# Two-layer gated cross attention with experts: value products joined per key tile, maxima as single evenly placed units, exponentials 800 columns wide

## The reference

```python
x = x + tanh(g_xattn[0]) * L0_xattn(layernorm(x), ctx, ctx, mask)     # 16 heads of 8, masked softmax
x = x + tanh(g_ffn[0])   * L0_ffn(layernorm(x))                       # 64 experts, 8 per token, and a shared one
x = x + tanh(g_xattn[1]) * L1_xattn(layernorm(x), ctx, ctx, energy)   # softmax times a gate per key
x = x + tanh(g_ffn[1])   * L1_ffn(layernorm(x))                       # 8 experts, 2 per token
```

## Time and profile before

| what | us |
|---|---|
| median of 3 runs | 1134.18 (1134.06 to 1135.10) |
| the profiled execution | 1136.61 |
| its span, first to last instruction | 1134.80 |
| TensorE, VectorE, ScalarE busy in it | 1000.3, 821.4, 564.5 |
| opening maxima, layer 0 and layer 1 | 28.0 and 22.5 |
| one batch of attention, layer 0 and layer 1 | 52.6 to 54.2 and 41.6 |

### The profile page before, as it was taken

How to read it: one execution, slowest core, us unless ns; L and a number is a source line. 1 busy time by engine, 2 the same in 40 slices (tenths; PEclk the granted TensorE clock), 3 DMA queues, 4 the chain that set the end, 5 groups by cost and what they waited for, 6 DMA issues and landing times.

```text
span 1134.8 us, 25320 instructions
## 1 busy us (share of the span) xinstructions
PE 1000.3 (88%) x9740; PEld 704.2 (62%) x9740; DVE 821.4 (72%) x1911; ACT 564.5 (50%) x1194; POOL 351.3 (31%) x278
## 2 busy tenths in 40 slices
PE   4889999999999999858999789999999999960997
PEld 2356666666666666548888546666666666540986
DVE  7977776767767675657999797777777677440996
ACT  2034445454544446525666306665655655750664
POOL 6521221212130300005777450441341341000774
PEclk8579999999999999958999859999999999975999
DMA  6522313030303040017655143223313404005662
GB/s 170 103 46 55 76 38 80 28 80 28 80 28 81 1 108 2 2 51 203 172 166 151 36 113 79 67 67 81 82 51 80 97 11 108 2 5 89 181 166 59
DMA packets 48094, 88.57 MB, mean 78 GB/s; under 512 B 21154, under 2 KB 31558, under 8 KB 47974
## 3 DMA queue, kind: packets, MB, share of 16 engines
q1 hardware_dynamic: 47974, 86.96, 31.6%
HBM read 47.24 MB, written 1.75 MB: 43 GB/s over the span
## 4 chain that ended last, share of the span: by engine, by line
PE 56%; DVE 18%; issue 6%; POOL 6%; ACT 4%; DMA 4%; SPq 1%; DVEq 0%; POOLq 0%; ACTq 0%
PE pm L1130 15%; PE po L1176 14%; PE ps L1156 11%; POOL tmpf L775 6%; PE ps L1159 5%; PE pc L1087 4%; DVE junk L416 3%; PE pc L1104 3%; DVE vaug L537 2%; DVE qsel L528 2%; ACT qsel L939 2%; DVE mx_part L419 2%; DMA routing<-vaug 2%; DVE negm L429 2%; DMA wts<-in_experts 1%
## 5 line engine op out<-in xcount | busy, mean ns | idle before, releaser
L851 ACT ACTIVATE probs<-ps 121x400 f32<-121x400 f32 (+1 forms) x768 | 347.7, 503 | 264.0 <-PE ps L1159 168.2
L1130 PE MATMUL pm<-khi,qbd 128*100 128x482 f32 (+5 forms) x653 | 318.5, 496 | 12.1 <-DVE mx_part L416 8.7
L416 DVE CUSTOM_DVE_ANT_0 junk<-pm,negq 100x482 bf16<-100x482 f32 (+1 forms) x360 | 233.3, 658 | 79.3 <-PE pm L1130 58.4
L1156 PE MATMUL ps<-qst,kst 128*121 128x400 f32 (+1 forms) x768 | 259.7, 404 | 5.5 <-ACT probs L851 2.9
L419 DVE TENSOR_REDUCE mx_part<-pm 128x1 f32<-128x482 f32 (+3 forms) x293 | 186.0, 655 | 58.7 <-PE pm L1130 57.4
L1176 PE MATMUL po<-probs,vaug 121*32 121x100 f32 x6144 | 214.2, 258 | 3.9 <-ACT oraw L878 3.9
L1176 PEld LDWEIGHTS po<-probs,vaug 121*32 121x32 f32 x6144 | 128.6, 110 | 116.3 <-issue 99.9
L1130 PEld LDWEIGHTS pm<-khi,qbd 128*100 128x100 f32 (+2 forms) x653 | 115.8, 179 | 86.3 <-issue 42.8
L1156 PEld LDWEIGHTS ps<-qst,kst 128*121 128x121 f32 (+1 forms) x768 | 141.4, 188 | 42.4 <-issue 20.7
L1301 PE MATMUL ps<-qsel,qst 128*128 128x400 f32 x660 | 139.9, 364 | 1.1 <-DVE qst L520 1.1
L775 POOL TENSOR_TENSOR tmpf<-vaug,wb 128x400 f32<-128x400 f32 x55 | 68.6, 1248 | 213.1 <-DMA wb<-routing 151.5
(11 more groups left out here) (179 smaller groups left out, 1011.2 us busy)
## 6 DMA issues: line engine op xcount, KB each, us to landing
kst<-khi SPq DMA_DIRECT2D x128, 180.5 KB, 3.9
wb<-routing SPq DMA_DIRECT2D x66, 200.0 KB, 3.7
ctxT<-in_ctxT SPq DMA_DIRECT2D x16, 722.0 KB, 4.2
kst<-klo SPq DMA_DIRECT2D x64, 180.5 KB, 3.9
wts<-in_experts SPq DMA_DIRECT2D x55, 192.0 KB, 3.7
wb<-routing SPq DMA_DIRECT2D x22, 400.0 KB, 4.0
qsel<-qhi SPq DMA_DIRECT2D x16, 100.0 KB, 2.5
routing<-vaug SPq DMA_DIRECT2D x1, 1100.0 KB
```

The costliest lines, as they stand in the source:

```text
L416: ins = nc.vector.tensor_tensor_reduce(junk[:, k % 2, 0:w], max_bank(b, k)[0:S, 0:w], negq[:, lo:lo + w], 1.0, -3e38, ALU.add, ALU.max, mx ...
L851: nc.scalar.activation(probs[t % 2][0:r, g * GQ:(g + 1) * GQ], ps[0:r, g, 0:GQ], ACT.Exp, scale=SCALE).then_inc(s["probs_ready"], 1)
L1130: nc.tensor.matmul(max_bank(b, k)[0:rows, 0:w], qbd[:, first:first + rows], khi[:, lo:lo + w], start=True, stop=True).then_inc(s["chunk_re ...
L1156: mm = nc.tensor.matmul(ps[0:r, g, 0:GQ], kst[par][:, g, t * KEY_TILE:t * KEY_TILE + r], qst[par][:, g * GQ:(g + 1) * GQ], start=True, sto ...
```

## The change

- `weigh` does a key tile's sixteen value products in one run, behind scores 0 and 1 of the next tile, and waits for all its exponentials.
- The exponential covers two groups, 800 columns, at once (`exp_half`). A score group waits for the half that last used its bank pair.
- The due times go. Maxima are single units: one behind each score, a fifth (if the tile has one) behind the product placed beside. A unit is now (block, third); the thirds start at 0, 482 and 962 and are all 482 wide, and in layer 1 the last block overlaps so that all have 128 rows. All use the two banks of `pm`, those of batch 0 too.
- `khi`, `klo` and `qbd` have two buffers. K of batch b+2 is projected in tiles 4 to 6 of batch b, K of batch 1 among the opening maxima; V in tiles 7 to 9; `turn_out`, `turn_back`, `project` in tiles 1, 2 and 3.
- The sign of the maximum is in `max_mask`; the negation goes. The gate is multiplied into `wo` and, with the bias, into `xres` ahead of the layer's first maximum, and `add_out` is one operation. The semaphore increment ahead of each layer-0 maximum on VectorE goes.

```diff
-MAX_PER_SLOT = [[1, 4, 4, 4, 4, 4, 4, 5, 6, 6, 6, 0], [0, 4, 4, 3, 3, 3, 3, 4, 5, 5, 5, 0]]
+UNITS_PER_SLOT = [[5, 4, 4, 4, 5, 4, 4, 4, 5, 5, 4, 0], [4, 4, 4, 4, 4, 4, 4, 3, 3, 3, 2, 0]]
+TURN_OUT_SLOT, TURN_BACK_SLOT, OUT_SLOT, K_SLOT, V_SLOT, ROW_SLOT = 1, 2, 3, 4, 7, KEY_TILES - 1
+FIRST_K_AFTER, FIRST_K_TAKEN = [7, 15, 23], [11, 19, 27]
...
-                        dve.sem_inc(s["chunk_seen"], 1)
...
-                    nc.vector.tensor_scalar(negm[0:rows, 96:96 + blocks], negm[0:rows, 96:96 + blocks], -1.0, None,
-                                            ALU.mult).then_inc(s["rowmax_step"], 1)
...
+                step(nc.vector.tensor_scalar(wo[l][:], wo[l][:], tgates[:, l:l + 1], None, ALU.mult))
+                step(nc.vector.scalar_tensor_tensor(xres[:], bo[l][0:S, :].unsqueeze(1).broadcast_to([S, B, D]),
+                                                    tgates[0:S, l:l + 1], xres[:], ALU.mult, ALU.add))
...
+                    nc.scalar.activation(probs[t % 2][0:r, 2 * u * GQ:2 * (u + 1) * GQ].rearrange("p (g q) -> p g q", q=GQ),
+                                         ps[0:r, 2 * u:2 * u + 2, 0:GQ], ACT.Exp, scale=SCALE)\
...
+                    if n >= 2:
+
+                        pe.wait_ge(s["max_taken"], n - 1)
+                    first, lo = MAX_FIRST[l][i], MAX_STARTS[c]
+                    nc.tensor.matmul(pm[0:rows, n % 2, 0:MAX_W], qbd[b % 2][:, first:first + rows],
+                                     khi[b % 2][:, lo:lo + MAX_W], start=True, stop=True).then_inc(s["chunk_ready"], 1)
...
-                    pe.wait_ge(s["probs_ready"], b * (G * KEY_TILES) + (G * t + 2 * u + 2))
+                    pe.wait_ge(s["probs_ready"], 2 * (b * KEY_TILES + t) + 2)
...
+                        scores(b, t, 0)
+                        for u in here[0:1]:
+                            max_unit(b + 1, u)
+                        if b < B - 1 and t == ROW_SLOT:
                             max_rows(b + 1)
...
+                        scores(b, t, 1)
+                        for u in here[1:2]:
+                            max_unit(b + 1, u)
+                        if t >= 1:
+                            weigh(b, t - 1)
+                        elif b >= 1:
+                            weigh(b - 1, KEY_TILES - 1)
+                        scores(b, t, 2)
+                        for u in here[2:3]:
+                            max_unit(b + 1, u)
+                        scores(b, t, 3)
+                        for u in here[3:4]:
+                            max_unit(b + 1, u)
+                        beside(b, t)
+                        for u in here[4:]:
+                            max_unit(b + 1, u)
+
+                for u in range(len(units)):
+                    max_unit(0, u)
+                    if u in FIRST_K_AFTER:
+                        k_chunk(1, FIRST_K_AFTER.index(u))
...
-    a["max_mask"] = (row[:, None] - 96 == np.arange(H)).astype(f)
+    a["max_mask"] = -(row[:, None] - 96 == np.arange(H)).astype(f)
...
-    nc = bacc.Bacc("TRN2", target_bir_lowering=False, num_devices=1)
+    nc = bacc.Bacc("TRN2", target_bir_lowering=False, num_devices=1, dynamic_dma_scratch_size=1024)
```

More of the change, by code:

```diff
@@ L184, in flamingo @@
         ctxT = [sb(f"ctxT{i}", [128, NKP]) for i in range(2)]
-        khi = sb("khi", [128, NK], F32R)
-        klo = sb("klo", [128, NK], F32R)
+        khi = [sb(f"khi{i}", [128, NK], F32R) for i in range(2)]
+        klo = [sb(f"klo{i}", [128, NK], F32R) for i in range(2)]
         kst = [sb(f"kst{i}", [128, G, NK], F32R) for i in range(2)]
@@ L193, in flamingo @@
         qst = [sb(f"qst{i}", [128, HQ], F32R) for i in range(2)]
-        qbd = sb("qbd", [128, HQ], F32R)
-        mx_part = sb("mx_part", [128, H, len(CHUNKS)])
+        qbd = [sb(f"qbd{i}", [128, HQ], F32R) for i in range(2)]
+        mx_part = sb("mx_part", [128, H * 3])
         negm = sb("negm", [128, 128])
-        junk = sb("junk", [100, 2, 512], BF16)
+        junk = sb("junk", [100, 2, MAX_W], BF16)
         probs = [sb(f"probs{i}", [KEY_TILE, HQ]) for i in range(2)]
@@ new lines, in unit_max @@
+                def unit_max(b, u):
+                    n, (i, c) = b * len(units) + u, units[u]
+                    bank = pm[0:rows, n % 2, 0:MAX_W]
+                    part = mx_part[0:rows, i * 3 + c:i * 3 + c + 1]
+                    dve.wait_ge(s["chunk_ready"], n + 1)
+                    if l == 1:
+                        nc.vector.tensor_reduce(part, bank, AX, ALU.max).then_inc(s["max_taken"], 1)
+                    else:
+                        nc.vector.tensor_tensor_reduce(junk[:, n % 2, :], bank, negq[:, MAX_STARTS[c]:MAX_STARTS[c] + MAX_W],
+                                                       1.0, -3e38, ALU.add, ALU.max, part).then_inc(s["max_taken"], 1)
@@ L432, in row_max @@
+                def row_max(b):
+                    parts = mx_part[0:rows, 0:blocks * 3].rearrange("p (h c) -> p h c", c=3)
+                    dve.wait_ge(s["max_taken"], (b + 1) * len(units))
+                    nc.vector.tensor_reduce(negm[0:rows, 96:96 + blocks], parts, AX, ALU.max)\
+                        .then_inc(s["rowmax_ready"], 1)
                     dve.wait_ge(s["maxrow_ready"], b + 1)
-                    if not (isinstance(b, int) and b < 2):
-                        dve.wait_ge(s["pv_done"], b * KEY_TILES - KEY_TILES)
@@ L480, in slots @@
-                def slots(b, main, tail, par):
-                    for t in range(KEY_TILES):
-                        if main and t == 0:
-                            k_low(b + 1, 0)
-                        for i, k in enumerate(MAX_SLOTS[l][t]):
-                            chunk_max(b + 1, k)
-                            if i == BESIDE_AFTER.get(t, 0):
-                                beside(b, t, main, tail)
-                        if tail and t == OUT_SLOT:
-                            add_out(b - 1)
-                    row_max(b + 1, 1 - par)
@@ L686, in max_queries @@
                 def max_queries(b):
-                    if not (isinstance(b, int) and b == 0):
-                        pool.wait_ge(s["chunk_ready"], b * (3 * MAX_BLOCKS[l]))
-                    nc.gpsimd.tensor_tensor(qbd[:].rearrange("p (h q) -> p h q", q=S),
+                    if b >= 2:
+                        pool.wait_ge(s["chunk_ready"], (b - 1) * len(MAX_UNITS[l]))
+                    nc.gpsimd.tensor_tensor(qbd[b % 2][:].rearrange("p (h q) -> p h q", q=S),
                                             qhi[:, bass.ds(b * S, S)].unsqueeze(1).broadcast_to([128, H, S]),
@@ L903, in slots @@
                                 router0("a")
-                slots(0, True, False, True, 0)
+                for c in range(len(CHUNKS)):
+                    k_high(1, c)
+                slots(0)
                 if l == 0:
@@ L1291, in attention @@
+                for u in range(len(units)):
+                    max_unit(0, u)
+                    if u in FIRST_K_AFTER:
+                        k_chunk(1, FIRST_K_AFTER.index(u))
+                max_rows(0)
+                for b in range(B):
+                    slots(b)
+                weigh(B - 1, KEY_TILES - 1)
+                turn_out(B - 1)
                 turn_back(B - 1)
```

373 lines of the change are left out of this document (136 added, 237 removed).

## The result

The changed kernel takes **1105.93 us** (median of 4 runs, 1102.24 to 1108.05) against 1134.64 of the kernel before on the same chip: ratio **0.9744**, 95% interval 0.9716 to 0.9771. It is 28.7 us faster, two and a half times the forecast gain of 11.4. That lies inside the range of 1102 to 1140, but outside the 1112 to 1134 that the forecast claimed on its own. The profiled execution is the fastest of the four (span 1100.4) and that of the kernel before is 2 us over its median, so differences of the two traces come out some 6 us too good.

The account below looks back on a forecast made before the run. TensorE's stream was taken to bound the batches and VectorE the openings. Layer 0 at -20.8 us and layer 1 at +9.4 gave net -11.4, so 1123 us; range 1102 to 1140, about 8 in 10, 1112 to 1134 on its own.

Parts of the forecast that it names:

- the openings: Opening stretches: two banks for four +8.1 and +7.2 us, K of batch 1 +4.8 per layer, new operations +2.0 and +1.7.
- the five low clocks of layer 0: Layer-0 batch edges: the low clock behind five row-maxima waits goes, -8.0 us.
- the row wait: Layer-0 batch edges: with the negation gone TensorE waits 0.87 us instead of 1.84, -5.2 us over the layer.
- The slow rival: Layer-1 batches: stops of 0.2 to 0.6 us lower the clock, 1.6 us per drop, 1145 at two per batch; chance 12%.
- The scaling of `wo`: Ahead of VectorE's first maximum: this tensor_scalar beside GpSimd's work could be caught for up to 1.6 us.
- the openings at the full clock: Rival for the opening stretches: 0.62 us per maximum and K at 0.81, -16 us, 1107; chance 12%.
- banks that don't bind: Rival for layer 1: VectorE catches up in the value run, 3.5 us per batch go, 1099; chance 10%.
- the 0.5 that I had put on top for VectorE's start: Layer-0 batches: a further instruction at VectorE's start on a maximum costs 0 to 0.5 us per batch, 0.5 taken.
- banks 3.48: Layer-1 batch: waits for the two maxima banks to turn round, summed over its tiles, lose 3.48 us.
- -29.4 for joining: Batches 0 to 6, each layer: joining value halves saves 0.355 us per key tile, 4.25 per batch of twelve, 29.4 in all.
- +29.9 for banks and exponentials: Layer-1 batches 0 to 6: bank waits and 800-column exponentials cost 4.4 us in six batches, 3.6 in batch 0.
- Batch 7: Layer 1, no maxima: the 800-column exponential makes a cycle of 2.46 us against 2.1, +4.4 us.

Follow-up runs that it names:

- `a4`: The changed kernel with four banks again for the maxima of batch 0, in both layers: 1089.03 us, 0.9595 of the kernel before.
- `b1`: The kernel before with its maxima spread more evenly over the tiles, all else as before: 1137.58 us, 1.0026 of the kernel before.
- `b2`: The kernel before with the sign of the maximum in the mask and the negation taken out: 1110.84 us, 0.9789 of the kernel before.
- `a1`: The changed kernel with each tile's value products in two halves again: 1140.61 us, 1.0046 of the kernel before.
- `b3`: The kernel before with each tile's value products in one run, its own maxima kept: 1140.49 us, 1.0060 of the kernel before.
- `a5`: The changed kernel with GpSimd's masked queries for the next maxima ahead of the values in its list: 1099.77 us, 0.9693 of the kernel before.
- `c1`: The changed kernel with VectorE reducing only 241 of 482 columns per layer-1 maximum, so outputs are wrong: 1078.89 us, 0.9513 of the kernel before.
- `a2`: The changed kernel with exponentials of 400 columns again, one per score group: 1105.10 us, 0.9737 of the kernel before.
- `a3`: The changed kernel with the negation back on VectorE and the sign out of the mask: 1109.04 us, 0.9767 of the kernel before.
- `d1`: The changed kernel with four banks for batch 0's maxima and masked queries made a batch earlier: 1081.87 us, 0.9536 of the kernel before.
- `d2`: `d1` with VectorE taking K's low part behind the tile's second maximum instead of ahead of the first: 1077.08 us, 0.9494 of the kernel before.
- `d3`: `d2` with layer 1's order behind the value run made maximum, score, maximum, score: 1071.49 us, 0.9450 of the kernel before.
- `e1`: `d3` with the energy gates' addition of one as scalar_tensor_tensor instead of tensor_scalar: 1072.42 us, 0.9450 of the kernel before.

## Why the prediction was right or wrong

**Right.** TensorE's stream sets the batches and VectorE the openings. The joined run takes 0.83 us, the openings came out within 2 us of their terms, the five low clocks of layer 0 went, the row wait fell from 1.84 to 0.66 (forecast 0.87), the plain layer-1 tile is 3.22 for 3.24. Two banks for four cost 17 us by `a4` (15.3 in the sum for the banks alone, the K products apart; the 0.757 of layer 1's price stands there without its working, but its 7.2 us for 39 products are near the 7.6 of `a4`). The slow rival, a clock falling in layer 1 at stops of 0.2 to 0.6 us, didn't happen: behind the opening's low clock there is one drop, 3.4 us in batch 6, and its stop was 1.26 us. The rule on short idles at the PSUM banks that the prediction quotes from the Trainium skill ("TensorE: Matmul & The Clock Gate", section "A second HAM failure mode: psum-queue depth-cycling") didn't show itself at this size of stop. The scaling of `wo` was caught beside GpSimd, as the prediction allowed: 1.20 and 1.18 us for 128 columns, each ending 0.08 us behind a GpSimd instruction; with the new residual operation (1.28 and 2.08) the two took 2.5 and 3.3 us for 2.0 and 1.7, inside their bounds. The rivals whose times lie nearest (1107, the openings at the full clock; 1099, banks that don't bind) did not happen: the openings' clock is 0.54 and 0.67, and the banks bind.

**Wrong: the batches of layer 0, -45.1 for -34.0.** The step that failed is that of making the sum by differences from the measured batch. Built up from the pieces of the prediction, a layer-0 batch is twelve tiles of 3.27, K 3 x 0.81, V 3 x 0.7, the turns 0.8, the row maxima's product and wait 1.2, the banks 0.8: 46.6 us; the trace has 47.20, four times over. By differences it came to 341.0 / 7 = 48.7. What the differences left standing were the three stops in the V tiles (1.2 per batch, fence of `b1`), which belong to the old order and went with it, and the 0.5 that I had put on top for VectorE's start isn't there either.

The runs divide a plain layer-0 batch without a low clock like this; the wait for the row maxima is gone in the first two steps, and 0.66 us of it come back with the last:

| step | from, to | measured | forecast's terms |
|---|---|---|---|
| the negation out | 52.6 (before), 50.8 (`b2`) | -1.8 | -1.0 (rows) |
| all the rest but joining | 50.8, 50.2 (`a1`) | -0.6 | +0.4 (start of maxima, K) |
| the value run joined | 50.2, 47.2 (changed) | -3.0 | -3.4 (joining, banks) |

The largest miss is the middle step, in which the maxima become single. From 100 to 400 us TensorE stops for a bank of the maxima 18 times in the kernel before (4.8 us in all), 23 times with the run joined alone (`b3`, 6.4), and with single maxima among halves (`a1`) once, 1.9 us, at the gates. So the stops went with the single maxima and not with the joined run.

A second, smaller error is one of counting. K of batch b+2 is projected in batch b, so batch 6 has no K at all, and its three products (2.4 us per layer) stayed in my sum while K of batch 1 was added in the opening. Batch 6 is 45.4 us for 47.2 in layer 0, and in layer 1 37.1 for 39.1 (`a5`, where no low clock falls into it). With 1.5 us per plain batch, this and a batch 0 shorter by 1.0 than the others on one side and the 2.3 of the gates on the other, the 11.1 us are accounted for.

**Right in sum, and there in part by luck: layer 1, -10.5 for -7.3.** The same step failed here too. Built up from the prediction's pieces (twelve tiles of 2.60, less nine maxima of 0.20, K, V and turns as above, 0.3 for the row product, banks 3.48, exponentials 0.9; an estimate made afterwards) a batch is 39.4 us, and `a5`, without the queries' wait, has 39.1; by differences it was 41.6 - 7.3 / 7 = 40.6. What hid the error is a wait that the forecast doesn't have, the 1.26 us for GpSimd's queries at six edges. -29.4 for joining and +29.9 for banks and exponentials were to leave nothing of it, and `a1` puts joining, net of both, at 2.6 us per batch: the losses at K's low part that I charged to the joined run stand in the order with halves as well. The plain tile, the banks (`c1`) and the exponentials' waits at the edges (`a5`) came out; `a2` gains nothing at the edges, since GpSimd's queries held TensorE longest. Batch 7 is +2.0 for +4.4: its tiles take 2.38, not 2.46, which is 1.0 of the 2.4; the rest is not placed.

**Missed in both directions.** The queries' wait in layer 1, above, and the energy gates ahead of a tile with five maxima, 2.3 us in the changed kernel: the old order had one maximum in that tile and hid them. And one low clock in layer 1, behind the last of the six stops of 1.26 us.

**The negation, priced too low and counted as its own.** `b2` finds 17.5 us in the batches of layer 0, 4.4 in those of layer 1 and 2.4 in the openings; my 5.2 + 8.0 in layer 0 let a wait of 0.87 stand, which is the new order's. In the changed order the negation would hardly have waited for GpSimd (`a3`, 3 us): two edits each remove the same cost, so their single values don't add.

**Left open.** Routing and experts of layer 0 are 6.2 us shorter for 1.2. The stretch with the routing is 22.2 to 24.5 us in the changed kernel and its eleven variants and 25.2 to 26.3 in the four kernels of the old order, so they differ by 0.7 us at least; the experts' stretch is 128.0 to 131.9 in the one and 130.0 to 132.3 in the other, which overlap. Why the routing is shorter no run shows.

## What to carry to other kernels

Build a changed stretch from its pieces, and set that sum against the one made by differences; here it was the better one in both layers. What the pieces of the old order can't explain may be the old order's own waits, and need not be inherited. For every instruction that is put earlier in a tile, read what stood before it on the engine that feeds it; the three costs missed here (queries on GpSimd, gates and K's low part on VectorE) were all work that an empty first tile had hidden. A short VectorE instruction on SBUF data beside GpSimd's long ones is to be looked up by its duration in the trace, and moved or folded away.

## What the runs showed of the hardware

- An instruction of VectorE with 16 columns took 0.17, 0.25 or 1.82 us, one with 96 columns 0.21, 0.36, 2.79 and (as scalar_tensor_tensor) 2.84, by where GpSimd stood. It can wait through four GpSimd instructions in a row, and not only to the end of the one that runs. The Trainium skill ("SBUF — State Buffer", section "SBUF: two separate sides") has the pair of ports locked for a whole instruction; who comes next between two of GpSimd's that section doesn't say, and the runs show both.
- One size of stop doesn't settle whether the granted clock falls. It fell behind a stop of 1.84 us at five edges of six in the kernel before, behind 1.50 at two of six in `b3`, behind 1.26 once of six in the changed kernel (895.4 to 898.8, above) and never behind the 0.66 of layer 0's edges. The stop of 2.03 us at the gates brought no low clock in the changed kernel and 3.4 us of it in `a2`, `a3` and `c1`; that of 4.5 us brought 3.4 in `d1` and 6.8 in `a5`, `d2`, `d3` and `e1`.
- One exponential of 800 columns out of two banks takes 0.84 us, two of 400 take 0.50 each, 0.90 together.
